# A graph network with additive attention on one core: score groups in cycles of two packed and one scalar, other TensorE work between the packed ones

## The reference, cut to what matters

```python
# x: (8, 2048, 128), adj: (8, 2048, 2048), all float32; ln is a layer norm over the last axis
x = ln(x + gcn(x, adj, W0, b0))           # layer 0: normalised adjacency times x, then a 128x128 weight
q, k = x @ WQ, x @ WK                     # layer 1: additive attention
h = relu(q[:, None, :, :] + k[:, :, None, :])
score = einsum('bijd,d->bij', h, p)       # 8 x 2048 x 2048 scores, each a sum over 128 channels
x = ln(x + softmax(score + mask(adj)) @ x)
x = ln(x + gcn(x, adj, W2, b2))           # layer 2
x = ln(x + gcn(x, adj, W3, b3))           # layer 3
```

## Time and profile before

| | us |
|---|---|
| median of 3 runs | 13932.96 |
| lowest and highest | 13930.92, 13934.58 |
| the profiled execution | 13921.96 |
| its span, first to last instruction | 13920.2 |

### The profile page before, as it was taken

The page is one execution under the profiler, slowest core; times in us unless marked ns, Lnnn a source line. Parts: engine busy times, 40 slices in busy tenths (PEclk is TensorE's granted clock), DMA queues, the critical chain, the costliest instruction groups (busy, mean ns, idle before and its releaser), DMA issues.

```text
span 13920.2 us, 320252 instructions
## 1 busy us (share of the span) xinstructions
PE 12944.8 (93%) x143877; PEld 6304.3 (45%) x143877; DVE 12353.1 (89%) x8531; ACT 12465.2 (90%) x8292; POOL 11710.4 (84%) x6447
## 2 busy tenths in 40 slices
PE   7889989999899998999989999899998999999998
PEld 3444434444444444444444444444444444444443
DVE  6998998889988899888998889988899888998995
ACT  5999998899988999889998899988998889999994
POOL 4888888888888888888888888888888888888884
PEclk9999999999999999999999999999999999999999
DMA  4111112221122212222122211222112222111103
GB/s 143 52 46 48 52 57 82 86 64 48 61 82 89 61 43 65 85 88 61 38 74 82 87 57 45 68 85 84 56 45 73 82 83 62 36 47 56 43 16 110
DMA packets 752100, 918.85 MB, mean 66 GB/s; under 512 B 62608, under 2 KB 511120, under 8 KB 748688
## 3 DMA queue, kind: packets, MB, share of 16 engines
q1 hardware_dynamic: 750736, 898.36, 21.0%
HBM read 705.23 MB, written 184.55 MB: 64 GB/s over the span
## 4 chain that ended last, share of the span: by engine, by line
PE 57%; ACT 18%; DVE 17%; POOL 6%; issue 2%; DMA 1%; SPq 0%; POOLq 0%; DVEq 0%; ACTq 0%
PE score L1247 42%; ACT scalar_rows L908 16%; DVE pair_rows L1088 15%; PE acc L1163 8%; POOL pair_rows L688 5%; PE turn L1134 3%; PE acc L1224 2%; PE acc L1181 1%; DVE q_pair L1016 0%; DMA piece<-adj_turned 0%; DVE gx L997 0%; PE acc L1169 0%; ACT q_pair L808 0%; PE turn L1193 0%; ACT att_turned L884 0%
## 5 line engine op out<-in xcount | busy, mean ns | idle before, releaser
L688 POOL TENSOR_SCALAR pair_rows<-q_pair,k_pair_cols 128x2050 f32<-128x2050 f32 x5628 | 11036.4, 1980 | 1855.6 <-PE score L1247 1827.5
L1088 DVE TENSOR_SCALAR pair_rows<-q_pair,k_pair_cols 128x2050 f32<-128x2050 f32 x4864 | 11076.7, 2341 | 1287.0 <-PE score L1247 1272.6
L908 ACT ACTIVATE scalar_rows<-q_f,k_cols 128x2048 f32<-128x2048 f32 x5808 | 11159.1, 2004 | 231.9 <-PE score L1247 222.0
L1247 PE MATMUL score<-pair_rows,unit_window 128*32 128x512 f16 x83936 | 5467.1, 396 | 713.7 <-DVE pair_rows L1088 560.6
L1247 PE MATMUL score<-scalar_rows,sign_window 128*32 128x512 f32 x46464 | 5424.5, 596 | 153.4 <-ACT scalar_rows L908 152.1
L1247 PEld LDWEIGHTS score<-pair_rows,unit_window 128*32 128x32 bf16 x83936 | 2873.8, 97 | 3452.7 <-issue 1043.0
L1247 PEld LDWEIGHTS score<-scalar_rows,sign_window 128*32 128x32 f32 x46464 | 1810.9, 110 | 2981.2 <-issue 2602.2
L1163 PE MATMUL acc<-piece,q_f 128*128 128x512 f32 x2944 | 1411.8, 602 | 17.0 <-DMA piece<-adj_turned 15.3
L808 ACT ACTIVATE q_pair<-turn 128x512 f32<-128x512 f32 x448 | 262.1, 585 | 765.5 <-PE turn L1134 765.5
L1163 PEld LDWEIGHTS acc<-piece,q_f 128*128 128x128 f32 x2944 | 502.6, 190 | 529.9 <-issue 469.1
L1224 PE MATMUL acc<-x,att_turned 128*128 128x128 f32 x4096 | 560.1, 280 | 0.0
(11 more groups left out here) (101 smaller groups left out, 2664.9 us busy)
## 6 DMA issues: line engine op xcount, KB each, us to landing
piece<-adj_turned SPq DMA_DIRECT2D x1472, 256.0 KB, 2.8
q_pair<-in_adj_dram SPq DMA_DIRECT2D x240, 512.0 KB, 4.6
adj_turned<-q_pair SPq DMA_DIRECT2D x224, 512.0 KB, 4.9
att<-in_adj_dram SPq DMA_DIRECT2D x128, 820.0 KB, 4.9
att<-in_adj_dram SPq DMA_DIRECT2D x128, 204.0 KB, 5.1
q_f<-in_adj_dram SPq DMA_DIRECT2D x16, 512.0 KB, 5.5
gx<-in_x_dram SPq DMA_DIRECT2D x32, 256.0 KB, 3.9
adj_turned<-pair_rows SPq DMA_DIRECT2D x8, 1024.0 KB, 11.3
```

What stands on the lines that cost most here:

```text
L688: ins = pool.tensor_scalar(slot_row(n, g, u), pairs_of(c + 1), 3.0e38, k_pair_cols[:, t % 2, QUAD * u + g:QUAD * u + g + 1], ALU.min, ALU.max)
L908: ins = nc.scalar.activation(slot_row(n, g, u)[:, 0:N], q_of(c + 1), ACT.Relu, bias=k_cols[:, t % 2, QUAD * u + g:QUAD * u + g + 1])
L1088: ins = nc.vector.tensor_scalar(slot_row(n, g, u), pairs_of(c + 1), k_pair_cols[:, t % 2, QUAD * u + g:QUAD * u + g + 1], None, ALU.max)
L1247: ins = nc.tensor.matmul(score[QUAD * u:QUAD * (u + 1), cc, :], (unit_window if pair else sign_window)[:, QUAD - 1 - g:2 * QUAD - 1 - g], ...
```

## The change

- The scalar groups, of which 12 stood evenly in a block (11 with units), get lists by kind of block: 10 in a block with a step, 11 with units alone, 12 with neither. Up to group 16 every third group is scalar.
- DPPP groups and lent rows have new places and numbers.
- All tables of places move, PE's so that its other work stands at the second packed group of a pair. The 16 pieces of a step start at -7 in pairs.
- ACT's copies out of PSUM, its copies of the weights and its exponentials stand between the second and third row of a scalar group (`MID_ROW`), not ahead of the first row or behind it.
- `SPARE_AT`, `THIN` and `ROOTS_BLOCK` name block 9 with units. The last unit starts in block 8 under both versions, so neither table is ever used.

```diff
-    N_ACT = 12
-    SCALAR_GROUPS = [(a * GROUPS + GROUPS - 2) // N_ACT for a in range(N_ACT)]
-    LEFT_OUT = 5
+    SCALAR_GROUPS = {"steps": (2, 5, 8, 11, 14, 17, 20, 23, 27, 31),
+                     "units": (2, 5, 8, 11, 14, 17, 20, 23, 26, 29, 31),
+                     "plain": (2, 5, 8, 11, 14, 17, 19, 22, 24, 27, 29, 31)}
     RING = 2
...
-    SLOTS = [0, 6, 10, 14, 18, 23, 28]
-    EVICT = {0: 4, 6: 9, 10: 13, 14: 17, 18: 22, 23: 27, 28: 31}
-    SUM_UNIT = {0: 3, 6: 8, 10: 12, 14: 16, 18: 21, 23: 25, 28: 33}
+    SLOTS = [1, 4, 10, 19, 22, 25, 29]
+    EVICT = {1: 5, 4: 8, 10: 14, 19: 23, 22: 27, 25: 31, 29: 34}
+    SUM_UNIT = {1: 6, 4: 9, 10: 15, 19: 18, 22: 28, 25: 32, 29: 35}
     BLOCK = {"layer2": 2, "layer3": 6, "layer0": 10}
-    PIECES_AT = {-4: [0, 1, 2], 0: [3, 4, 5], 1: [6], 4: [7], 10: [8, 9], 14: [10], 18: [11], 23: [12, 13, 14, 15]}
-    SELF_AT, TURNED_AT, PROJECT_AT, SUM_AT, ROOT_AT, NORM_OUT_AT, STORE_AT = 18, 28, 28, 31, 33, 40, 41
-    SCALE_AT = {"layer2": [-25, -20, -15, -10], "layer3": [-5, -3, -1, 11], "layer0": [-5, -3, -1, 16]}
-    BIAS_AT, FIRST_LOAD_AT = 20, -8
-    QK = {"turn": 46, "copy": 49, "q": 50, "q_out": 54, "k": 55, "q_store": 56, "q_split": 58, "k_out": 59,
-          "q_high": 61, "k_store": 61, "q_pair_store": 62, "k_split": 76, "k_high": 78, "k_pair_store": 79}
-    X1_AT, X2_AT, X0_AT = 28, 34, 45
+    PIECES_AT = {-7: [0, 1], -6: [2, 3], -3: [4, 5], -2: [6, 7], 1: [8, 9], 4: [10], 7: [11], 13: [12], 16: [13], 19: [14, 15]}
+    SELF_AT, TURNED_AT, PROJECT_AT, SUM_AT, ROOT_AT, NORM_OUT_AT, STORE_AT = 16, 24, 22, 26, 28, 30, 31
+    SCALE_AT = {"layer2": [-25, -20, -15, -10], "layer3": [-8, -7, -6, 2], "layer0": [-8, -7, -6, 6]}
+    BIAS_AT, FIRST_LOAD_AT = 20, -12
+    QK = {"turn": 39, "copy": 43, "q": 42, "q_out": 46, "k": 45, "q_store": 48, "q_split": 49, "k_out": 49,
+          "q_high": 53, "k_store": 51, "q_pair_store": 54, "k_split": 56, "k_high": 60, "k_pair_store": 61}
+    X1_AT, X2_AT, X0_AT = 25, 30, 34
     DIAG_AT, DEGREE_AT, DIS_AT, KEEP_AT = 9 * GROUPS - 16, 9 * GROUPS + 8, 9 * GROUPS + 9, 11 * GROUPS + 9
...
-        TURN_AT = {6: 0, 10: 1, 14: 2, 18: 3}
-        COPY_IN = {10: 0, 13: 1, 18: 2, 23: 3}
-        MULTIPLY_AT = {10: 0, 14: 1, 18: 2, 23: 3}
-        MASK_AT, EXP_AT, NORM_AT, ATT_ROOT_AT, OUTPUT_AT = 24, 5, 27, 28, 31
-        MASK_LOAD_AT, K_LOAD_AT = 19, 21
+        TURN_AT = {4: 0, 7: 1, 10: 2, 13: 3}
+        COPY_IN = {8: 0, 11: 1, 14: 2, 17: 3}
+        MULTIPLY_AT = {7: 0, 10: 1, 13: 2, 16: 3}
+        MASK_AT, EXP_AT, NORM_AT, ATT_ROOT_AT, OUTPUT_AT = 22, 5, 20, 21, 24
+        MASK_LOAD_AT, K_LOAD_AT = 14, 21
+        MID_ROW = 2
...
-        SPARE_AT = 9
-        THIN = (8, 9, 11, 12, 14)
-        THIRD_ROWS = {(True, True): (1, 25, 30), (True, False): (1, 25), (False, True): (1, 9, 25, 30), (False, False): (1, 25)}
-        LENT_ROWS = [(18, 3), (7, 3)]
+        ROOTS_BLOCK = 9
+        THIRD_ROWS = {"steps": (1, 3, 21, 24, 28), "units": (1, 3, 21, 25), "roots": (1, 28), "plain": (1, 3, 21, 28)}
+        LENT_ROWS = [(11, 3), (23, 3)]
+
+        def sort_of(c, t):
+            if units_in(c, t) and t == ROOTS_BLOCK:
+                return "roots"
+            return "steps" if step_in(c, t) else "units" if units_in(c, t) else "plain"
 
         def kinds(c, t):
-            return ["A" if g in SCALAR_GROUPS and (g != LEFT_OUT or not units_in(c, t)) else "D" for g in range(GROUPS)]
+            groups = SCALAR_GROUPS[{"roots": "units"}.get(sort_of(c, t), sort_of(c, t))]
+            return ["A" if g in groups else "D" for g in range(GROUPS)]
 
         def units_in(c, t):
             return len(units_where(c, lambda u: slot_place(2 * u) // GROUPS == t)) > 0
@@ -273,11 +279,8 @@
 
         def makers(c, t, g):
             if kinds(c, t)[g] == "A":
-                lent = LENT_ROWS[:1 if step_in(c, t) else 2] if units_in(c, t) else []
-                return "".join("P" if (g, u) in lent else "A" for u in range(P // QUAD))
-            if units_in(c, t) and t == SPARE_AT and g in THIN:
-                return "DDDP"
-            return "DPPP" if g in THIRD_ROWS[units_in(c, t), step_in(c, t)] else "DDPP"
+                return "".join("P" if sort_of(c, t) == "units" and (g, u) in LENT_ROWS else "A" for u in range(P // QUAD))
+            return "DPPP" if g in THIRD_ROWS[sort_of(c, t)] else "DDPP"
...
-            def side(c, place):
+            def copies(c, place):
                 for k in range(2):
                     for u in units_where(c, lambda u: evict_place(2 * u + k) == place):
                         copy_unit(c, u, k)
+                queries_keys(c, place)
+
+            def side(c, place):
                 for u in units_where(c, lambda u: sum_place(u) == place):
                     sum_unit(c, u)
                 for name, s in steps_at(c, place, TURNED_AT):
                     turn_layer(c, name, s)
                 if place == DEGREE_AT and not one_of(c, LAST, CLOSING):
                     diag_sizes(c)
-                queries_keys(c, place)
...
                     n = block_of(c, t)
-                    if before and g == EXP_AT:
-                        exponentials(n)
...
                         act.wait_ge(rows_used["A"], GROUP_NO[n, g] + 1)
-                        for u in range(P // QUAD):
-                            if before and u == 1 and g in COPY_IN:
+                    for u in range(P // QUAD):
+                        if u == MID_ROW:
+                            if before and g == EXP_AT:
+                                exponentials(n)
+                            if before and g in COPY_IN:
                                 copy_weights(c * T + (T + t - 1), COPY_IN[g])
-                            if MAKERS[n, g][u] != "A":
-                                continue
+                            copies(c, place)
+                        if MAKERS[n, g][u] == "A":
                             ins = nc.scalar.activation(slot_row(n, g, u)[:, 0:N], q_of(c + 1), ACT.Relu,
                                                        bias=k_cols[:, t % 2, QUAD * u + g:QUAD * u + g + 1])
+                    if KINDS[n, g] == "A":
                         ins.then_inc(rows_ready["A"], 1)
 
             for u in range(UNITS):
                 first_unit(u)
             for place in range(PLACES):
```

More of the change, by code:

```diff
@@ L47, in build @@
     PITCH = PART + 2
-    assert PARTS % 2 == 1 and PART * PARTS == N + 2 and PART % 2 == 0 and LEFT_OUT in SCALAR_GROUPS
+    assert PARTS % 2 == 1 and PART * PARTS == N + 2 and PART % 2 == 0
     HALF = N // 2
@@ L412, in scored @@
         def scored(n):
-            return groups_through(n - 1, SCALAR_GROUPS[-1]) + RING
+            return groups_through(n - 1, GROUPS - 1) + RING
         def flat(tiles):
@@ L915, in _ @@
                 side(OPENING, place)
+                copies(OPENING, place)
             attention(FIRST)
@@ L924, in _ @@
                 side(CLOSING, place)
+                copies(CLOSING, place)
         @block.vector
```

## The result

The changed kernel takes 13,710.22 us (median of 4 runs, 13,702.39 to 13,713.41), the kernel before 13,931.94 beside it (4 runs, 13,928.39 to 13,934.58): 0.984 times as long, 95% interval 0.9823 to 0.9857, 222 us less. I forecast 13,495, 437 less. The span of the profiled execution is 13,700.3 us, against 13,920.2.

A forecast was written before the change was run, and what follows sets the result against it. No single engine was taken as the bound: PE, DVE and POOL wait for each other through a two-group ring. Gains by kind of block summed to 436 us, taking 13,922 to 13,486, forecast 13,495; range 13,320 to 13,800.

The forecast's parts named there:

- rival "half": Places 24 to 4: ring only half full, POOL 48 us against PE 42, 252 us less gain; 13,620 to 13,850, chance 0.22.
- Full blocks: 42 blocks with units and a step: PE 102.5 plus 1.5 exposed and 0.7 for chance, 104.7 from 110.7; gain 252 us.
- Units alone: Blocks with units, no step: 99.5 from 103.9 in pass -1 (gain 40), 101.5 from 105.9 later (gain 53).
- neither: 14 blocks without units or step: ACT's 96.4 is the bound, 98.0 from 100.1, gain 30; last pass nothing.
- The block's start: Group 0 overwrites scores DVE must first read, now uncovered: 1 to 2 us per block exposed, taken as 1.5.
- The chain of a step: PE's projection at 22, ACT's copy at 24: ACT needs 8.8 us, PE 11.4, so hidden by 2.6 us.
- the slower rival: PE's projection at 22 waits for ACT's copy at 24, up to 5.0 us in 84 step blocks, 420 us; chance 0.12.
- three at one height: 103.2 from 104.4: 28 blocks with a step alone: PE 100.4, DVE 100.0, POOL 99.7, taken as 103.2 from 104.4; gain 34 us.
- Block 9: POOL at 109.5 becomes the bound; 109.8 from 112.4, gain 16 us for six, plus 3 in pass -1.
- ACT's waits: In full blocks ACT's 93.2 us of waits for turned units would fall to near nothing, with copies in mid-group.
- Signs that I named: Full blocks 104 to 105 us, DVE's and POOL's waits under half; wrong if PE waits for POOL or block 9 lengthens.
- The insertions: PE's other work at 12 places for 9: three more insertions in 84 step blocks at 0.34 us, 86 us.

The follow-up runs named there:

- experiment 4: Changed kernel with PE's other work one place later everywhere, rows, makers and ACT's places unchanged: 14,009.11 us, ratio 1.0056 to the kernel before.
- Experiment 1: Changed kernel with 11 scalar groups for 10 and four DPPP groups for five in blocks with a step but no units: 13,643.62 us, ratio 0.9793.
- Experiment 3: Changed kernel with ACT's copies and exponentials ahead of a scalar group's first row (MID_ROW 0 for 2): 13,902.49 us, ratio 0.9977.
- experiment 6: Changed kernel with the first eight pieces in fours at two places (-7 and -3), not in pairs at four: 13,829.27 us, ratio 0.9929.
- experiment 7: Changed kernel with the DPPP groups of step blocks at 1, 3, 9, 15, 21 for 1, 3, 21, 24, 28: 13,937.08 us, ratio 1.0008.
- combined version: Changed kernel with 11 scalar groups in step-alone blocks (12 in block 9), k's split at 73, scalings spread, pieces 8 and 9 at place 0: 13,627.57 us.
- 5: Changed kernel with pieces 8 and 9 at place 0 and not at place 1: 13,690.95 us, ratio 0.9831.
- 10: Changed kernel with POOL's four scalings of layers 3 and 0 spread out, at -8, -5, -1, 5 (6): 13,697.97 us, ratio 0.9839.
- experiment 12: Changed kernel with 11 scalar groups for 10 and four DPPP groups for five in blocks with units and a step: 13,704.67 us, ratio 0.984.
- Experiment 8: Changed kernel with DVE's split of k at place 70 for 56 (second product 72, store 73): 13,877.21 us, ratio 0.9964.

## Why the prediction was right or wrong

**The number.** 13,710 lies in my range, but outside the forecast's own 13,380 to 13,620 and inside the range of the rival "half". The gain is half of what I put, so that the range holds is owed to the rival and not to the sum.

**Right.** *The sign, and where the gain is from.* Full blocks give 196 of the 222 us in the table. That the place of PE's work makes it was argued in the prediction; experiment 4 shows that the gain needs it: the same instructions one place later cost 299 us. A part of these comes through ACT, whose copies stand nearer in that run.

*The loads.* I had PE 102.5, POOL 99.6, DVE 98.0, ACT 91.5 in a full block; the window gives 103.1, 99.8, 98.6 and 91.0. In a block with a step alone I had PE 100.4, DVE 100.0, POOL 99.7; it is 101.0, 101.9 and 100.5.

*Units alone*, 99.2 for 99.5, and *neither*, 97.0 for 98.0. *The block's start*: exposed, as I said, by 4.2 us in 7 full blocks and 4.7 in blocks 10 to 13, so 0.6 and 1.2 us, not 1.5. *The chain of a step*: PE's projection waited for ACT's copy 0.7 us at the most, as before the change, so the slower rival's mechanism was not there.

**The step that failed** is the term "three at one height: 103.2 from 104.4" for blocks with a step alone. The loads were nearly right and the block took 107.3, 5.4 us above its busiest engine. I had added 2.8 to that engine in the place where three engines are close, hardly more than the 2.2 of full blocks, where PE stands alone. In fact three engines at one height wait for each other in a ring of two groups: PE waited at 22 to 28 and at group 0, DVE and POOL waited 20.7 and 25.8 us, and ACT, the one that could have taken rows, idled 102.3. Experiment 1 shows that what was moved from ACT to DVE and POOL is one cause (55 us in these blocks and the last pass). That the closeness of the three loads makes the rest is argued and not shown: 2.6 us a block over the forecast remain, most of them in blocks 11 and 12, for which no experiment found a cause.

**Terms that were mis-sized.** *Full blocks*, 1.3 us each: PE is 2.9 us short of the block, of which 2.0 is its wait for POOL's rows, most of it at group 28, and 0.6 that at group 0. *Block 9*: my own sum had POOL at 109.5; it is busy 112.16 of 112.8, though experiment 1 shows that less load for POOL alone does not shorten the block. *Opening and closing*: 8 us longer.

**Half right: ACT's waits.** I wrote that its wait for turned units would be near nothing. It is 88.5 us for 93.2 before, only for another reason (the store of the unit before, not PE's turning). What I had right is the cover: in mid-group the wait costs PE next to nothing (0.2 us for ACT's rows). Experiment 3 prices that at 192 us. The prediction gave the copies no term of their own, and with the copies ahead of the rows there is nearly no gain. The parts don't add up: undoing the place costs 299 us, the copies 192, the pairs 119, the places of POOL's rows 227, of a gain of 222. I read it so that each keeps the cycle even, and one that breaks it lets the waits in again; no run tests that reading by itself.

**Signs that I named.** DVE's waits for PE fell to 57% and not to under half, ACT's wait for turned units stayed, and the full blocks took 106.0 us, not 104 to 105. Of the signs of being wrong two came: PE waits for POOL's rows at group 28, and block 9 became 0.4 us longer.

**The insertions.** I charged 86 us for three more insertions a block, at 0.34 us each. The rows that I named give less: 1.19 us for a piece alone and 1.81 / 2 = 0.91 in company make 0.28, so 71 us. PE's busy time in the full blocks is 103.1 for my 102.5, which doesn't contradict either. One thing that an insertion gives back I left out: the pair at place 30 covers the block's start, and without it and the pair at 26 the program is 119 us slower (experiment 6). Two readings in the prediction were loose besides. Before the change the work at places 14 and 28 stood ahead of packed groups and not of scalar ones, and the lower bound leaves the 1.5 us out for block 9 and the blocks with neither; neither moves the forecast.

**The rival "half"** gave 13,620 to 13,850, and 13,710 lies in it. Its place was right: in full blocks PE waits for POOL at 28. Its cause was not the whole: it blamed POOL's four DPPP groups in the stretch from 24 to 4, and moving two of them out (experiment 7) only made PE wait for DVE. So what is short in that stretch is DVE and POOL together. The prediction says itself that its sum needs a full ring at place 24 in every block; that condition deserved more than 0.22 against 0.50.

**Open.** In the combined version blocks with a step still stand 2.4 us (full) and 4.2 us (alone) above their busiest engine. The gains of experiments 1, 5 and 10 and of block 9 don't add up in it, and experiment 12 moved load without moving time. Whether a deeper ring would free this wasn't tried.

## What to carry to other kernels

Where several producers feed one consumer through short rings, put the consumer's other work in small, even pieces between two groups of the slowest producer; moving it by one place cost 299 us here. See too that something covers the moment at which the consumer must wait for its own results to be read. Look twice at loads levelled to the last per cent while another engine waits: here a block with three engines within 2% of each other stood 5.4 us above the busiest, against 2.9 where one led, and giving rows back to the waiting engine won 67 us; but in the blocks where one engine led, the same move won nothing (experiment 12). An in-order engine's copy that may wait for a transfer stands cheaper in the middle of a batch than ahead of it, since half the batch is made while the transfer runs.

## What the runs showed of the hardware

DVE's bitwise operation from SBUF to SBUF (L1019, 128x512) takes 0.42 us alone, and much longer when POOL makes rows from SBUF at the same time. The changed kernel's timeline of DVE and of POOL, block 11 of pass 1:

```profile
4714.60 0.42 DVE L1019 TENSOR_SCALAR q_pair<-q_pair 128x512 int32<-128x512 int32 x1
...
4735.00 1.48 DVE L1019 TENSOR_SCALAR q_pair<-q_pair 128x512 int32<-128x512 int32 x1
4736.51 2.44 DVE L1025 TENSOR_TENSOR q_pair<-q_pair 128x512 f16<-128x512 f32 x1
```

```profile
4732.26 10.44 POOL L691 TENSOR_SCALAR pair_rows<-q_pair,k_pair_cols 128x2050 f32<-128x2050 f32 x5
```

Here POOL's second row ends at about 4732.26 + 2 x 1.95 = 4736.2 and DVE's operation 0.3 us later: it waited for the row under way. The Trainium skill, SBUF — State Buffer, section Who interferes with whom, has the same for those DVE instructions that use the pair of ports shared with GpSimd: whoever issues first keeps it for the whole instruction. Experiment 8 goes further than that: the operation stood 10.24 us, over five of POOL's rows, until the unbroken run of 21 ended. There the measurement decides: rows of POOL that follow each other without a pause can hold DVE off for longer than one instruction. When it is one row and when the whole run, these traces don't tell.
